# A DLRM tower on one core: pairs turned by whole-array transposes, the last product on 32-column quarters, products between the last block's fills

## What is computed

```python
e = stack([tbl_f[ids[:, f]] for f in range(26)], axis=1)      # (2048, 26, 128)
combined = concatenate([e, dense[:, None, :]], axis=1)        # (2048, 27, 128)
z = einsum('bfd,bgd->bfg', combined, combined)[:, I, J]       # 351 pairs, i < j
h = concatenate([z, dense], axis=1)                           # 479 columns
h = maximum(h @ W_top1 + b_top1, 0)                           # 512
h = maximum(h @ W_top2 + b_top2, 0)                           # 256
y = h @ W_top3                                                # 1
```

## Time and profile before

| what | us |
|---|---|
| median of 3 runs | 390.56 (390.32 to 392.99) |
| the profiled execution, its own time | 390.03 |
| its span, first to last instruction | 388.2 |
| time outside the span | 1.83 |
| PE busy | 354.7 of 388.2 |
| POOL busy | 264.9 of 388.2 |

### The profile page before, as it was taken

The page is one execution under the profiler, slowest core; times in us unless marked ns, Lnnn a source line. Parts: engine busy times, 40 slices in busy tenths (PEclk is TensorE's granted clock), DMA queues, the critical chain, the costliest instruction groups (busy, mean ns, idle before and its releaser), DMA issues.

```text
span 388.2 us, 14394 instructions
## 1 busy us (share of the span) xinstructions
PE 354.7 (91%) x6432; PEld 321.3 (83%) x6432; DVE 222.7 (57%) x253; ACT 174.0 (45%) x483; POOL 264.9 (68%) x280
## 2 busy tenths in 40 slices
PE   2887979998999999999999999998999989989787
PEld 2776868987889888988889888888989888978676
DVE  4786898944568535763568535763568534821122
ACT  2437236545436173544436273444446253453422
POOL 6777787767777777777777777777777777773000
PEclk9999999999999999999999999999999999998999
DMA  6777415323232323232222322223231322221000
GB/s 177 234 221 210 120 46 136 71 78 82 63 84 56 82 65 85 56 82 52 80 68 58 83 63 84 57 76 85 69 84 50 83 65 55 58 57 37 2 3 0
DMA packets 17566, 31.25 MB, mean 80 GB/s; under 512 B 5720, under 2 KB 8672, under 8 KB 17504
## 3 DMA queue, kind: packets, MB, share of 16 engines
q0 software_dynamic: 8704, 17.84, 18.4%
q1 hardware_dynamic: 7920, 11.68, 10.0%
q10 hardware_dynamic: 880, 0.80, 0.7%
HBM read 30.29 MB, written 0.01 MB: 78 GB/s over the span
## 4 chain that ended last, share of the span: by engine, by line
PE 78%; DMA 8%; DVE 5%; ACT 5%; issue 3%; SPq 0%; ACTq 0%; DVEq 0%
PE x_ps L618 34%; PE tail_ps L702 16%; PE gram_ps L637 13%; DMA hot_in<-in_tbl 8%; PE x_ps L599 6%; DVE onehot L894 3%; PE tail_ps L662 3%; PE tail_ps L674 2%; ACT xt L394 2%; PE tail_ps L708 2%; DVE hot_lo L880 1%; ACT xt L841 1%; ACT gram L416 1%; PE x_ps L742 1%; PE tail_ps L753 0%
## 5 line engine op out<-in xcount | busy, mean ns | idle before, releaser
L582 POOL DMA_INDIRECT raw<-in_tbl,ids_sb x272 | 264.1, 971 | 88.8 <-issue 82.4
L894 DVE TENSOR_TENSOR onehot<-ids_wide,row_ps 128x1024 fp32r<-128x1024 int16 (+1 forms) x160 | 180.5, 1163 | 61.9 <-PE x_ps L618 58.1
L618 PE MATMUL x_ps<-onehot,hot_hi 128*128 128x256 f32 x566 | 147.1, 295 | 4.0 <-DVE onehot L894 1.3
L618 PE MATMUL x_ps<-onehot,hot_lo 128*128 128x256 f32 x566 | 139.7, 282 | 0.4 <-issue 0.4
L618 PEld LDWEIGHTS x_ps<-onehot,hot_hi 128*128 128x128 f32 x566 | 106.6, 188 | 11.7 <-ACT xt L394 3.9
L618 PEld LDWEIGHTS x_ps<-onehot,hot_lo 128*128 128x128 f32 x566 | 106.7, 188 | 0.5 <-issue 0.5
L394 ACT COPY xt<-x_ps 128x128 f32<-128x128 f32 (+1 forms) x99 | 47.8, 565 | 47.8 <-PE x_ps L618 47.2
L637 PE MATMUL gram_ps<-xt 128*27 128x26 f32 x4096 | 52.4, 192 | 9.6 <-issue 5.7
L637 PEld LDWEIGHTS gram_ps<-xt 128*27 128x27 f32 x4096 | 43.6, 104 | 18.7 <-issue 11.4
L599 PE MATMUL x_ps<-ident,raw 128*128 128x128 f32 x272 | 40.9, 279 | 7.8 <-ACT xt L394 7.2
L416 ACT COPY gram<-gram_ps 128x416 f32<-128x416 f32 (+1 forms) x32 | 16.2, 506 | 66.8 <-PE gram_ps L637 66.8
(11 more groups left out here) (90 smaller groups left out, 339.6 us busy)
## 6 DMA issues: line engine op xcount, KB each, us to landing
raw<-in_tbl,ids_sb POOLq DMA_INDIRECT x272, 2.6
ids_wide<-in_hot_ids SPq DMA_DIRECT2D x17, 256.0 KB
hot_in<-in_tbl SPq DMA_DIRECT2D x14, 256.0 KB, 3.5
weights_in_place<-in_w SPq DMA_DIRECT2D x12, 128.0 KB, 2.4
hot_in<-in_tbl SPq DMA_DIRECT2D x4, 320.0 KB, 4.0
dense_sb<-in_dense_t ACTq DMA_DIRECT2D x6, 128.0 KB, 2.6
dense_sb<-in_dense_t SPq DMA_DIRECT2D x2, 128.0 KB, 4.1
ids_wide<-in_hot_ids SPq DMA_DIRECT2D x1, 192.0 KB
```

Of the source, the lines that this page charges most:

```text
L582: nc.gpsimd.indirect_dma_start(out=raw[k][:, f, :], out_offset=None, in_=sources[f], in_offset=bass.IndirectOffsetOnAxis(ap=ids_sb[:, t, f ...
L618: last = nc.tensor.matmul(ps, table[:, chunk_at[j] + c, :], moving[:, c - a, :], start=(c == 0 and table is tables_of[0]), stop=(c == chun ...
L894: nc.vector.tensor_tensor(columns(p), ids_wide[:, it // IDS % IDS_RING, it % IDS, 0:width].unsqueeze(1).to_broadcast([P, n, width]), row_n ...
```

## The change

- (zt, 0) turns the first 128 pairs of both halves at once: four transposes of 128x128 into one bank of 512 columns. (zt, 1) turns what is left into the other bank: four transposes of 64x64 (54 pairs and 10 padded columns of zeros, written once) and, on the other half of the rows, four fp32 matmuls with the identity, 41 wide. The third step and `rest_turned` are gone; the copies are one of 128x512 and one of 105x256 on ACT and on DVE. The first layer's parts are now 128, 128 and 105 pairs.
- `y` is eight matmuls of 64 columns, one for each quarter of the columns and each part of `h2`, into output rows 0, 32, 64 and 96; ACT copies 97x64 and the store takes four rows. In the order, `y` stands one slot later, in front of the next block's third fill.
- In the last block the first tile's two fills are parted by two slots that only tail steps of the block before can fill, and `last_start(0)` and `last_start(1)` stand between the last tile's two fills. The dense residue that the first of them needs is made there too.
- With one tail step fewer, all other tail steps move a little within their stretch.

```diff
-    rest = 64
-    z_blocks = [[(0, slice(0, half_pairs[0] - rest))], [(1, slice(0, P))],
-                [(1, slice(P - rest, half_pairs[1])), (0, slice(half_pairs[0] - rest, half_pairs[0]))]]
-    n_kz = len(z_blocks)
-    kz = [blk[0][1].stop - blk[0][1].start for blk in z_blocks]
-    assert sum(kz) == pairs and max(kz) <= P
+    z_wide = P + P // 2
+    assert sum(half_pairs) == pairs and P < half_pairs[1] <= half_pairs[0] <= z_wide
+    n_zt = 2
+    kz = [P, P, half_pairs[1] - P // 2]
+    n_kz = len(kz)
+    zt_of = [0, 0, 1]
     n_cols = len(col_groups)
-    tail = ([("cols", g) for g in range(n_cols)] + [("zt", k) for k in range(n_kz)]
+    tail = ([("cols", g) for g in range(n_cols)] + [("zt", k) for k in range(n_zt)]
...
-    parts = {(kind, j): len(z_blocks[j]) if kind == "zt" else len(cuts[kind]) - 1 if kind in layer else 1
+    parts = {(kind, j): len(cuts[kind]) - 1 if kind in layer else 1
...
-            slots += gram_slots(t) + with_turn([[] for _ in range(n)], t + 1, list(range(n)))
+            fills_of = gram_slots(t)
+            slots += fills_of[:1] + [[], []] + fills_of[1:] + with_turn([[] for _ in range(n)], t + 1, list(range(n)))
...
-        slots += gram_slots(t + 1, hot[lead:lead + beside])
+        slots += gram_slots(t + 1, hot[lead:lead + beside] if hot else [[("start", 0), ("start", 1)], []])
...
-            before.setdefault(tail_from[h] + min(int(at * n / span[-1]), n - 1), []).append(("tail", h, key, part))
+            place = n if key[0] == "y" else min(int(at * n / span[-1]), n - 1)
+            before.setdefault(tail_from[h] + place, []).append(("tail", h, key, part))
...
+        y_rows, y_cols = P // 4, BLOCK // 4
...
-        y_sb = sb("y_sb", [1, BLOCK])
+        y_sb = sb("y_sb", [P, BLOCK // 4])
...
-        z = sb("z", [P, QUAD, half_pairs[0]])
+        z = sb("z", [P, QUAD, z_wide])
...
-        last_y = gram_ps[0][0:1, 0:BLOCK]
+        last_y = gram_ps[0]
...
+        def zt_parts(j, ps, of):
+            if j == 0:
+                return (ps.rearrange("p (s o g) -> p o g s", s=QUAD, o=2),
+                        of[:, 0:2, :].rearrange("p o (g s) -> p o g s", s=QUAD))
+            return (ps[0:kz[2], 0:BLOCK].rearrange("p (s g) -> p g s", s=QUAD),
+                    of[0:kz[2], 2, :].rearrange("p (g s) -> p g s", s=QUAD))
+        def y_copy(act, h, ps):
+            reach(act, y_stored, 16 * h)
+            nc.scalar.copy(y_sb[0:3 * y_rows + 1, :], ps[0:3 * y_rows + 1, 0:y_cols]).then_inc(y_copied, 1)
+            act.wait_ge(y_copied, h + 1)
+        def y_store(act, h):
+            act.dma_start(out[:, h * BLOCK:(h + 1) * BLOCK].rearrange("o (s n) -> (o s) n", n=y_cols),
+                          y_sb[0:3 * y_rows + 1:y_rows, :]).then_inc(y_stored, 16)
...
-                src = ps[0:kz[j], 0:BLOCK].rearrange("p (s g) -> p g s", s=QUAD)
-                copy(zt_hi[0:kz[j], j, :].rearrange("p (g s) -> p g s", s=QUAD), src).then_inc(zt_rounded, 1)
+                src, hi = zt_parts(j, ps, zt_hi)
+                copy(hi, src).then_inc(zt_rounded, 1)
...
-                reach(act, y_stored, 16 * h)
-                copy(y_sb[:, :], ps[0:1, 0:BLOCK]).then_inc(y_copied, 1)
-                act.wait_ge(y_copied, h + 1)
+                y_copy(act, h, ps)
                 act.sem_inc(tail_copied[bank], 1)
-                act.dma_start(out[:, h * BLOCK:(h + 1) * BLOCK], y_sb[:, :]).then_inc(y_stored, 16)
+                y_store(act, h)
...
+        def dense_residue(dve, h):
+            dve.wait_ge(dense_rounded, h + 1)
+            nc.vector.tensor_tensor(dense_lo[h % DENSE][:, :], dense_sb[h % DENSE][:, :],
+                                    dense_hi[h % DENSE][:, :].bitcast(F32), ALU.subtract).then_inc(dense_split, 1)
...
-            if key == ("cols", 0):
-                dve.wait_ge(dense_rounded, h + 1)
-                nc.vector.tensor_tensor(dense_lo[h % DENSE][:, :], dense_sb[h % DENSE][:, :],
-                                        dense_hi[h % DENSE][:, :].bitcast(F32), ALU.subtract).then_inc(dense_split, 1)
+            if key == ("cols", 0) and h < blocks - 1:
+                dense_residue(dve, h)
             elif kind == "zt":
-                src = tail_ps[bank][0:kz[j], 0:BLOCK].rearrange("p (s g) -> p g s", s=QUAD)
-                hi, lo = (part[0:kz[j], j, :].rearrange("p (g s) -> p g s", s=QUAD) for part in (zt_hi, zt_lo))
+                (src, hi), (_, lo) = (zt_parts(j, tail_ps[bank], of) for of in (zt_hi, zt_lo))
                 nc.vector.tensor_tensor(lo, src, hi.bitcast(F32), ALU.subtract).then_inc(zt_split, 1)
...
+            def y_products(ps, c):
+                for s in range(4):
+                    last = nc.tensor.matmul(ps[s * y_rows:s * y_rows + 1, 0:y_cols], w3_sb[:, c:c + 1],
+                                            h2[:, c, s * y_cols:(s + 1) * y_cols], start=(c == 0), stop=(c == m2 - 1))
+                return last
...
-                if key == ("zt", 1):
-                    return
...
+                            pe.wait_ge(z_padded, 1)
...
-                    if part > 0:
-                        pe.wait_ge(rest_turned, h + 1)
-                    if j == 0:
-                        other = tail_bank["zt", 1]
-                        reach(pe, tail_copied[other], h * tail_per[other] + tail_nth["zt", 1])
-                    blocks_of = [z_blocks[0][0], z_blocks[1][0]] if j == 0 else [z_blocks[j][part]]
+                    upper, lower = slice(0, groups_block), slice(groups_block, P)
                     for s in range(QUAD):
-                        for bank_of, (odd, of) in zip((ps, tail_ps[tail_bank["zt", 1]]), blocks_of):
-                            rows = slice(odd * groups_block, (odd + 1) * groups_block)
-                            last = nc.tensor.transpose(
-                                bank_of[0:of.stop - of.start, s * groups_block:(s + 1) * groups_block],
-                                z[rows, s, of], ident[rows, rows])
-                            if s == QUAD - 1 and j == 0 and odd == 0:
-                                last.then_inc(tail_full[kind], 1)
-                    if part < parts[key] - 1:
-                        last.then_inc(rest_turned, 1)
+                        if j == 0:
+                            last = nc.tensor.transpose(ps[:, s * P:(s + 1) * P], z[:, s, 0:P], ident[:, :])
+                        else:
+                            of_s = slice(s * groups_block, (s + 1) * groups_block)
+                            nc.tensor.transpose(ps[0:P // 2, of_s], z[upper, s, P:z_wide], ident[upper, upper])
+                            last = nc.tensor.matmul(ps[P // 2:kz[2], of_s], z[lower, s, P:half_pairs[1]],
+                                                    ident[lower, lower], start=True, stop=True)
...
+                elif kind == "start":
+                    last_start(*what)
                 elif kind == "gram":
                     products(*what)
...
-            last_start(0)
             tail_step(h, ("cols", 0), 0)
             tail_step(h, ("cols", 1), 0)
-            last_start(1)
...
-            tail_step(h, ("zt", 2), 0)
-            for m in range(m1):
-                last_h1_with_hi(m, 0)
-            tail_step(h, ("zt", 2), 1)
+            for k in range(n_kz - 1):
+                for m in range(m1):
+                    last_h1_with_hi(m, k)
...
-                if k < n_kz - 2:
-                    for m in range(m1):
-                        last_h1_with_hi(m, k + 1)
...
-            for b, key in enumerate((("zt", 2), ("zt", 1))):
+            for b, key in enumerate((("zt", 0), ("zt", 1))):
...
-                last = nc.tensor.matmul(last_y, w3_sb[:, m:m + 1], h2[:, m, :], start=(m == 0), stop=(m == m2 - 1))
+                last = y_products(last_y, m)
...
-            act.wait_ge(y_stored, 16 * h)
-            copy(y_sb[:, :], last_y).then_inc(y_copied, 1)
-            act.wait_ge(y_copied, blocks)
-            act.dma_start(out[:, h * BLOCK:(h + 1) * BLOCK], y_sb[:, :]).then_inc(y_stored, 16)
+            y_copy(act, h, last_y)
+            y_store(act, h)
...
+            nc.vector.memset(z[0:groups_block, :, half_pairs[0]:z_wide], 0.0).then_inc(z_padded, 1)
...
+                elif kind == "start" and what == [0]:
+                    dense_residue(dve, blocks - 1)
...
-    rest = len(halves[0]) - 64
-    pair_rows = [halves[0][:rest], halves[1][:P], halves[0][rest:] + halves[1][P:]]
+    pair_rows = [halves[0][:P], halves[1][:P], halves[0][P:], halves[1][P:]]
...
-        "w1": np.concatenate([np.pad(w1[rows_of], ((0, P - len(rows_of)), (0, 0))) for rows_of in pair_rows]
+        "w1": np.concatenate([np.pad(w1[rows_of], ((0, -len(rows_of) % (P // 2)), (0, 0))) for rows_of in pair_rows]
```

37 lines of the change are left out of this document (18 added, 19 removed).

## The result

| | before | after |
|---|---|---|
| median of 20 runs each, us | 392.19 (390.32 to 395.45) | 389.13 (386.56 to 395.31) |
| the profiled execution | 390.03 | 390.03 |
| its span | 388.2 | 388.2 |
| last group of tile 15 turned at | 364.04 | 362.05 |
| from there to the end | 24.15 | 26.15 |

The ratio after/before is 0.9949, with a 95% interval of [0.9924, 0.9973]: 0.5% faster, some 2 us, where 7 were forecast. Time and range of the prediction both missed: 389.13 for 383.0, and above the 387.0 at which the range ended. The two profiled executions took the same time by chance: that of before lies 2.2 us under the median of its 20 runs, that of after 0.9 over its own.

A forecast was written before the change was run, and what follows sets the result against it. PE was taken to bound the kernel until gathers cap the gain: 13.7 us offered, 7.9 taken. Turn at 356.15 + 23.8 to the end + 1.2 clock = 381.15, with 1.83 outside 383.0 us; range 379.7 to 387.0.

The forecast's parts named there:

- the turns of the pairs: Twelve small passes at 0.6 us, turns 1.05 instead of 1.7 per block: 0.65 saved, 4.6 us in seven blocks.
- T: Start of the turn of tile 15's last group, forecast to go from 364.04 to 356.15 us.
- only the passes count: `y` ahead of a fill needing the same switch: 0.35 us instead of 1.15, 0.8 saved per block, 4.8 in six.
- The cap: Savings ahead of the turn of tile 15's last group are worth 7.9 us at most, then PE waits for gathers.
- the offer: Sum of savings ahead of tile 15's last turn: 4.8 + 1.15 + 4.6 + 3.2 = 13.7 us, 7.9 taken.
- the sign that the prediction named for being wrong: The forecast called itself wrong if PE never waits for a gather, or if POOL's pace changes.
- POOL's last gather unmoved: Sign of the forecast: POOL's last gather still starts at 353.6 us.
- The stalls: Waits inside fills at instruction-packet borders: tile 14's 1.63 us gone, 3.2 with clock; tile 15's last two fills each stall.
- rival 3: Last two fills run without a stall; second fill ends 2.0 us earlier, time 381.0 or 379.8; chance 0.16.
- From T to the end: Stretch behind tile 15's last turn: 24.15 + 0.9 - 0.7 - 0.6, say 23.8 us, plus 1.2 for the clock.
- the first two: Rivals with dearer small passes: PE stays the bound, 386.5 us at x = 0.075 per pass (0.16); or slower, 396 (0.04).
- The second: Rival: small passes in different quarters do not overlap, 0.13 us each, `y` 2.1; slower, 396 us; chance 0.04.

The follow-up runs named there:

- Experiment 2: Kernel after with the four 64x64 transposes first, then the other half's eight passes (the grouped turns): 384.84 us, ratio to before 0.9881.
- experiment 1: Each part alone on the kernel before: last product 392.87 us, ratio 1.0005; turns of the pairs 394.22, 1.0095; last block's order 390.78, 0.9989.
- experiment 3: 64 identity transposes (128 instructions) issued ahead of everything: on the kernel after 387.24 us, ratio 0.9854; on Experiment 2's kernel 384.31, 0.9838.
- experiment 6: First layer's three dense-vector products left out in blocks 0 to 6: on Experiment 2's kernel 380.65 us, ratio 0.9756; on the kernel after 383.17, 0.9824.
- experiment 4: Experiment 2's kernel with the two starts and the dense residue back where they were before: 387.30 us, ratio 0.9833.
- experiment 7: Kernel after with the old turns of the pairs (three steps, no padding): 389.71 us, ratio to before 0.992.

## Why the prediction was wrong

**The step that failed: the turns of the pairs.** "I take 0.6, near the 64-row transposes that alternate between halves" was the term. It measured 1.63, just beyond the upper end of the prediction's own 0.3 to 1.5. Experiment 2 shows that the order is most of it: the same instructions in another order take 0.91. The row that I took as nearest, eight transposes in 0.40, alternates between the halves of the array with one kind of instruction, and into two banks. The new step alternates between halves and, each time, between a transpose (one instruction pair) and an fp32 matmul (two), and both halves write into one bank. A transpose and its matmul cost 0.40 so, where grouped they cost (0.34 + 0.57)/4 = 0.23. Even grouped the step is 0.3 over the 0.6, so a part of the miss is the price of the passes themselves; and the four whole transposes took 0.53 for 0.45. Instead of 0.65 saved, 0.46 was lost per block: over seven blocks 7.8 us short of the 4.6 forecast, and in the last block 1.3 more (where the sum behind T had 0.9 for both turns, though its own terms make 1.05). The turns alone, in experiment 1, agree with it by their loss, 3.7 us by the ratio.

The Trainium skill (TensorEngine Tiling (Array Packing), Key Properties) says that different tiles can execute LdWeights and Matmul in parallel, and that changing the tiling mode drains TensorE. For the passes in four column groups the trace agrees with the first: 14 ns a pass in `y`. For the step at hand it doesn't: the transposes of one half and the matmuls of the other came one after another, 0.17 and 0.23. Whether a change between a transpose and a matmul counts as such a drain no run here tells, nor what the bank that both halves write has to do with it. A run with a bank for each half is missing.

**The last product: right in the sum of its passes, wrong in "only the passes count".** Forecast 0.35 a step, measured 0.23; but the fill behind takes 0.45 longer. 0.47 saved per block, six blocks, 2.8 us instead of 4.8, 2.0 short. The seventh, behind T, was free as forecast.

**The cap and the order of the limits: right, and not reached.** With the two terms as measured the offer was 2.8 + 1.15 - 3.2 + 3.3 = 4.05 us, under the 7.9 (3.3 is the stall of tile 14, 1.63, and the 1.7 of clock behind it); T came 2.0 earlier, and PE never waited for a gather, the sign that the prediction named for being wrong. Nearly all of the other 2.0 us stand in one wait, that of the turns for ACT's copies of the looked-up rows, in the kernel before and in that after:

```profile
PE x_ps L599 <- ACT xt L394: 7.2, 7, 1.6
PE x_ps L619 <- ACT xt L397: 9.1, 7, 1.8
```

It is 7.0 to 9.4 in the fourteen profiles and 8.6 where only the starts were changed, so it goes up and down without these edits, and the profile of the kernel before, 2.2 us under its median, had one of the low values. The stalls in the fills of the earlier blocks are 1.00 and 0.41 us in after and 0.57 and 0.94 in before, nearly the same in sum. That the gathers would cap a better version is what experiments 2, 3 and 6 showed, with T at 355.9 to 359.8, always 2.6 to 2.7 after the start of the last gather. "POOL's last gather unmoved" was wrong, though: its start wandered between 350.2 and 357.2, so this cap moves by itself by some us from one execution or kernel to the next. It is a floor of the moment, not 356.15.

**The stalls: right in place, half right in price.** The stall 227 instructions in is there, to one instruction, and with it the border a packet earlier, 29 ahead of the fill; so is the absence of the stall in tile 14 and the clock's return there. The stall took 1.44 us of 1.6 forecast. The second, forecast at T + 8.05, did not come; the starts ran at half clock and gave the packet its time, or it would have come earlier anyway: rival 3 for that half. (The two starts are 10 passes, 20 instructions and not the 24 of the forecast.) Experiments 3 and 4 confirm the model of 256 instructions, but its constant, 3.8 us from one crossing to the next packet's use, was 3.4 in after (365.99 - 362.58) and, in experiment 4, 2.4 (367.33 - 364.94) and then 3.5 (370.79 - 367.33). The Trainium skill (Runtime: NRT & Kernel Launch, Instruction fetch mechanics) calls the crossing mostly hidden. For most borders here it is: the kernel after has some 50 and PE shows six waits on "issue" in all, of 0.17 to 1.44 us. Where a border fell into fills it cost up to 2.5 us, 2.54 in the kernel before, with a clock stretch behind it in some places and not in others.

**From T to the end: 26.15 for 25.0.** `cols` at T + 9.84, where T + 9.0 and 1.2 of clock were forecast: 0.4 better. The turns and the first layer from 374.69 to 382.05, 7.36 for 6.1: 1.3 worse, and that is the failed term again. From the last `y` on it is 2.66 for 2.93 before, 0.3 of the 0.6 forecast, since its copy, store and their waits are nearly as long as before, and the second layer ahead of it takes 0.14 more: 0.5 worse. The transposes between `cols` and the turns, 0.2 better.

Together: 5.9 us short at T (362.05 for 356.15) and 1.15 behind it are the 7.05 by which the span was missed. Of the rivals, the first two (small passes dearer than thought) are nearest to what happened, though for the turns alone. The second priced each small pass at 0.13 us, which makes 12 x 0.13 + 0.6 = 2.16 for the turns, just what they took; but `y` took 0.23 where it had 2.1. One x was linked to both edits; they should have been two rivals. The time itself came out within 1% of before, to which the prediction gave 0.09.

**What stays open.** The parts don't add up: the ratios of the three in experiment 1 multiply to 1.009 where the whole change has 0.995, and the last product alone and all but the turns show none or little of the 2.8 us that the rows give the former. The term that failed is shown by its rows and by experiment 2; that without it the rest of the change would have gained what was forecast is not shown, and experiment 7 speaks against it. Each kernel has its borders, and with them stalls and clock stretches, elsewhere, and stretches at 1.2 GHz at 31, 96 and 134 us stand in the profiles of the last product alone and of all but the turns, and not in that of after. One stretch of 3.4 us costs up to 1.7 by the estimate of the prediction. I could not separate that from the edits; single effects under some 3 us in this kernel are read from rows, not from totals.

## What to carry to other kernels

Don't price a sequence of small TensorE instructions by a row that has the same sizes but one kind of instruction, or other banks: here the same twelve passes took 1.63 or 0.91 us by their order alone, so group transposes and group matmuls, and keep a run of one kind together on one half of the array. When a saving is placed directly ahead of a dense run of short instructions, measure the pair of them, not the step. And where the instruction stream has stretches of 256 instructions in little over 1 us, a change of some dozen instructions anywhere ahead of it can move stalls of 1 to 2.5 us in or out; two kernels should be compared with that in mind, and 128 idle instructions ahead are a cheap trial.

## What the runs showed of the hardware that I had not expected

- A 64x64 transpose followed by the two passes of a 41-wide fp32 matmul on the other 64 rows: 0.40 us for the three; four transposes together 0.34, eight passes together 0.57.
- Sixteen 64-column passes in four column groups take 0.22 us, and a fill of 128 passes directly behind them 2.17 us (mean of six) instead of 1.72. Behind four passes of 256 columns the fill keeps its 1.72 to 1.76.
- 128 instructions more, by moving one instruction packet's border out of a fill, shortened the profiled span from 388.2 to 385.6 us (medians 387.24 and 389.13, not run side by side).
- PE's granted clock fell to half for some 3.5 us not only behind stalls: in the profiles of experiments 3 and 6 in which PE waited 1.25, 2.09 and 1.34 us for the last gather, no fill behind it stalls, and the clock is at 0.50 within 4 us of the wait.
- POOL's 272 gathers show PE as what they waited for in none of the profiles but one (0.3 us, experiment 6), and still the last of them started at 350.2, 353.3, 354.9 and 357.2 us in four executions of four kernels. The waits of POOL, after and with the grouped turns and 128 instructions ahead (us in total, times, longest):

```profile
POOL raw L602 <- issue: 80.6, 261, 0.7
POOL raw L602 <- DMA raw<-in_tbl,ids_sb: 4.9, 10, 1.3
```

```profile
POOL raw L602 <- issue: 77.6, 252, 0.6
POOL raw L602 <- DMA raw<-in_tbl,ids_sb: 13.2, 19, 2.0
```

85.5 against 90.8 us of waits, the difference in waits for DMAs of the gathers themselves, and 263.4 against 265.0 busy: together 6.9 of the 7.0 us between the two ends. Why those DMAs took longer in one execution I haven't tried.
